# Second expert layer over sorted rows: dense experts replaced by 71 tiles of 128 rows of one expert

## What is computed

```python
x = x + window_attention(ln(x))                      # layer 0
t = x + experts0(ln(x))                              # 8 experts, top 2, renormalised gates
x = t + (whiten @ centred ln(t)) * gamma + beta      # layer 1: whitening by 3 Newton steps
# layer 1 experts: E = 8, H = 256, K = 2, on xf = ln(x), T = 4096 rows
probs = softmax(xf @ router_w + router_b)
topk_p, topk_i = top_k(probs, 2)                     # gates are these two, zero elsewhere
h = einsum('td,edh->teh', xf, w1) + b1
gated = silu(h @ wg + bg) * (h @ wv + bv)            # per expert, 256 wide
y = einsum('tef,efd->ted', gated, w2) + b2
out = einsum('ted,te->td', y, gates)
```

## Time and profile before

| | us |
|---|---|
| median of 3 runs | 1011.64 (1011.33 to 1014.1) |
| span of the profiled execution | 1014.5 |
| whitening matrix finished in it (end of L941) | 649.2 |
| first layer-1 expert matmul starts | 665.6 |

### The profile page before, as it was taken

The page is one execution under the profiler, slowest core; times in us unless marked ns, Lnnn a source line. Parts: engine busy times, 40 slices in busy tenths (PEclk is TensorE's granted clock), DMA queues, the critical chain, the costliest instruction groups (busy, mean ns, idle before and its releaser), DMA issues.

```text
span 1014.5 us, 18749 instructions
## 1 busy us (share of the span) xinstructions
PE 942.3 (93%) x6320; PEld 628.4 (62%) x6320; DVE 717.7 (71%) x1356; ACT 544.0 (54%) x866; POOL 564.8 (56%) x444
## 2 busy tenths in 40 slices
PE   6798999999999999999999997479999999999997
PEld 3465565665655656666656564357767767676675
DVE  3445657668576676775784554469899898998976
ACT  1232536636547457276474432147676676667764
POOL 5223365574564565655645543146767666677664
PEclk9797999999999999999999999579999999999999
DMA  6331000000000000000000000000000000000000
GB/s 242 104 100 68 1 2 1 1 2 1 3 1 3 2 1 2 1 2 1 2 1 1 1 1 0 0 1 1 11 1 11 11 0 10 0 10 0 10 11 11
DMA packets 4317, 16.07 MB, mean 16 GB/s; under 512 B 528, under 2 KB 656, under 8 KB 3856
## 3 DMA queue, kind: packets, MB, share of 16 engines
q1 hardware_dynamic: 3168, 12.20, 3.3%
q0 software_dynamic: 640, 2.10, 0.6%
q10 hardware_dynamic: 432, 0.76, 0.2%
HBM read 12.95 MB, written 2.10 MB: 15 GB/s over the span
## 4 chain that ended last, share of the span: by engine, by line
PE 71%; DVE 13%; issue 8%; ACT 4%; POOL 2%; DMA 1%; DVEq 0%; ACTq 0%; POOLq 0%
PE bank L1107 10%; PE bank L1082 10%; PE bank L1084 9%; PE bank L1083 9%; PE bank L988 7%; PE bank L1088 3%; PE bank L1103 3%; PE bank L997 3%; PE bank L1010 3%; DVE ym L647 2%; DVE hid_l L798 2%; PE bank L1104 2%; PE bank L1105 2%; DVE work L788 2%; PE bank L1173 1%
## 5 line engine op out<-in xcount | busy, mean ns | idle before, releaser
L456 POOL TENSOR_TENSOR work<-work 128x512 f32<-128x512 f32 x256 | 364.6, 1433 | 231.6 <-DVE work L792 115.9
L1082 PE MATMUL bank<-xh,Wh 128*128 128x512 f32 x512 | 235.3, 459 | 6.1 <-DVE work L788 3.8
L1084 PE MATMUL bank<-xh,Wl 128*128 128x512 f32 x512 | 201.9, 394 | 0.0
L1083 PE MATMUL bank<-xl,Wh 128*128 128x512 f32 x512 | 201.6, 394 | 0.0
L563 ACT ACTIVATE work<-bank 128x512 f32<-128x512 f32 x128 | 76.6, 598 | 155.3 <-PE bank L1084 153.9
L563 ACT ACTIVATE work<-bank,gv_bias 128x512 f32<-128x512 f32 x128 | 88.2, 689 | 108.7 <-PE bank L1084 107.9
L1107 PE MATMUL bank<-work,W 128*128 128x512 f32 x256 | 139.4, 627 | 6.1 <-ACT ob L588 4.8
L792 DVE TENSOR_TENSOR work<-work,bank 128x512 f32<-128x512 f32 x128 | 87.0, 684 | 77.0 <-ACT work L563 77.0
L798 DVE TENSOR_TENSOR hid_l<-work,hid_h 128x512 fp32r<-128x512 f32 x128 | 133.7, 1045 | 8.3 <-ACT hid_h L574 8.2
L431 POOL TENSOR_TENSOR Sx<-Sx,srec 128x1024 f32<-128x1024 f32 x32 | 61.9, 1933 | 119.3 <-DVE srec L688 119.3
L1082 PEld LDWEIGHTS bank<-xh,Wh 128*128 128x128 f32 x512 | 96.9, 189 | 45.6 <-issue 21.0
(11 more groups left out here) (167 smaller groups left out, 1463.4 us busy)
## 6 DMA issues: line engine op xcount, KB each, us to landing
work<-w1gv_dram SPq DMA_DIRECT2D x8, 640.0 KB, 4.0
work<-w_dram POOLq DMA_DIRECT2D x8, 256.0 KB, 3.3
W<-w_dram SPq DMA_DIRECT2D x2, 1024.0 KB, 6.3
out_dram<-X SPq DMA_DIRECT2D x8, 256.0 KB, 2.0
X<-x_dram SPq DMA_DIRECT2D x1, 1792.0 KB, 8.8
S<-small_dram ACTq DMA_DIRECT2D x1, 358.0 KB, 6.7
C<-const_dram SPq DMA_DIRECT2D x1, 356.0 KB, 5.9
qkv_w<-att_w_dram ACTq DMA_DIRECT2D x1, 320.0 KB, 4.5
```

Source lines behind the costliest of these rows:

```text
L456: pool.tensor_tensor(h2[:, u % 4, :], h[:, u % 2, :], csb[:, (u // FT) % 2, :], ALU.mult)\
L1082: mm(dst, wh, xh[:, p, :], start=True, stop=False)
L1083: mm(dst, wh, xl[:, p, :], start=False, stop=False)
L1084: last = mm(dst, wl, xh[:, p, :], start=False, stop=True)
```

## The change

The dense experts of layer 1 and `schedule_1` are gone. In their place `*_sparse` functions do this, all unrolled:

- Preparation is by units of 8 tiles (1024 tokens, two blocks). Its steps are listed in `PREP_STEPS`. Units 0 and 1 are prepared ahead of the first expert tile; unit 2 is spread over the steps 0 to 7 of the tile loop and unit 3 over 8 to 15. Each unit's two experts per token are picked on DVE (`pick_first`), the place of each row among the rows of its expert is counted by matmuls with a triangular matrix ("place"), and POOL writes each token's normalised row twice, once for each chosen expert, with its gate and its own address behind it, into a DRAM buffer `region` by 16 indexed DMAs of 128 rows. The last unit adds 8 such DMAs for padding.
- DVE makes a list of tiles (`dve_list`, 19 small operations on one partition): where each tile starts in `region`, and which expert it has. Groups of 8, 16, 16 and 31 tiles become free after units 0, 1, 2 and 3.
- SP loads each tile's 128 rows and its expert's b2 row into a ring of 8 buffers. PE and SP read start and expert from the list into registers, eight tiles at a time.
- For each tile PE transposes the rows, ACT and DVE split them, three matmuls of 512 columns make gate and value for 256 hidden columns, ACT applies silu, DVE multiplies by value and gate, PE transposes back, ACT copies, and two plain f32 matmuls with W2 give the output. DVE adds gate times b2, and POOL writes the 128 rows to their places in the DRAM buffer `results` by one indexed DMA.
- At the end SP reads `results` (4 MB), DVE adds two rows to each token, and SP stores.

In the set-up, the layer-1 bias goes into the fold: DVE first shifts w1 (`dve_w1`, four small operations for each expert) and `pe_fold` gets a third matmul with 8 rows; `pe_fold_bias` is gone and the filler matmuls run in its steps. The splitting of W2 is gone. Centring and normalising in layer 1 move from DVE to ACT. The core of the diff:

```diff
+MOE_GROUPS = (8, 16, 16, 31)
+TILES_MOE = sum(MOE_GROUPS)
+REGS = 8
+RING = 8
+PREP_STEPS = ("centre0", "centre1", "turn0", "turn1", "white0", "white1", "y0", "y1", "features0", "features1",
+              "logits", "route", "place", "list")
+PREP_AT = {2: (0, 0, 1, 1, 2, 2, 3, 3, 4, 4, 5, 5, 6, 7),
+           3: (8, 8, 9, 9, 10, 10, 11, 11, 12, 12, 13, 13, 14, 15)}
+        def sp_sparse(sp):
...
+                if t >= RING:
+                    sp.wait_ge(y_out[k], 16 * (t // RING))
+                sp.dma_start(rowbuf[:, k, :], region[bass.ds(starts[t % REGS], P), :]).then_inc(row_in[k], 16)
+                sp.dma_start(b2buf[:, k, :], b2[bass.ds(experts[t % REGS], 1), :].to_broadcast([P, P]))\
+                    .then_inc(row_in[k], 16)
+        def pool_step(u, name):
...
+                for j in range(UNIT):
+                    for k in range(2):
+                        at = where[:, u % 2, 2 * j + k:2 * j + k + 1]
+                        pool.indirect_dma_start(region, bass.IndirectOffsetOnAxis(ap=at, axis=0),
+                                                unit_rows(u)[:, j, k, :], None,
+                                                bounds_check=E * REGION + P - 1, oob_is_err=False)\
+                            .then_inc(sorted_in[u], 16)
+        def pool_sparse():
...
+                    pool.wait_ge(y_sb, t - 1)
+                    pool.indirect_dma_start(
+                        results, bass.IndirectOffsetOnAxis(ap=rowbuf[:, k, PLACE_AT:PLACE_AT + 1].bitcast(U32), axis=0),
+                        ysb[:, k, :], None, bounds_check=PAIRS - 1, oob_is_err=False).then_inc(y_out[k], 16)
+        def pe_rows(q):
+            if q >= 1:
+                pe.wait_ge(xl1_sb, q)
+            for t in range(2 * q, min(TILES_MOE, 2 * q + 2)):
+                pe.wait_ge(row_in[t % RING], 32 * (t // RING + 1))
+                last = nc.tensor.transpose(bank[:, TURN_X, (t % 2) * P:(t % 2 + 1) * P], rowbuf[:, t % RING, 0:P], ident)
+            last.then_inc(xt_ps, 1)
+        def pe_sparse():
...
+                    mm(bank[:, t % 2, :], low, wh, start=True, stop=False)
+                    mm(bank[:, t % 2, :], high, wh, start=False, stop=False)
+                    mm(bank[:, t % 2, :], high, wl, start=False, stop=True).then_inc(gu_ps, 1)
+                if t >= 2:
+                    r = t - 2
+                    pe.wait_ge(ht_sb, r + 1)
...
+                if t % 2 == 0 and t + 2 < TILES_MOE:
+                    pe_rows(t // 2 + 1)
+                if 1 <= t <= TILES_MOE:
+                    r = t - 1
+                    pe.wait_ge(hh_sb, r + 1)
...
+                for u, name in prep_steps(t):
+                    pe_step(u, name)
+        def dve_sparse():
...
+            for i in range(BLOCKS):
+                dve.wait_ge(fetched_in[i % 4], 16 * (i // 4 + 1))
+                for k in range(2):
...
+                    v.tensor_tensor(xb(i), xb(i), fetched[:, i % 4, :, k * P:(k + 1) * P], ALU.add).then_inc(x_sum, 1)
```

More of the change, by code:

```diff
@@ L63, in half_constants @@
     one = np.uint16(0x3F80)
-    return np.concatenate([np.eye(P), sel.reshape(P, E * P)], 1).astype(np.uint16) * one
+    before = np.triu(np.ones((P, P)), 1)
+    return np.concatenate([np.eye(P), sel.reshape(P, E * P), before, np.ones((P, P))], 1).astype(np.uint16) * one
+REGION = TOKENS + P
+PAIRS = 2 * TOKENS
+ROW, GATE_AT, PLACE_AT = 130, 128, 129
+OUT_OF_RANGE = 1 << 20
+UNIT = 8
+MOE_GROUPS = (8, 16, 16, 31)
+GROUP_AT = tuple(sum(MOE_GROUPS[:g]) for g in range(len(MOE_GROUPS)))
+GROUP_MAX = max(MOE_GROUPS)
+TILES_MOE = sum(MOE_GROUPS)
+REGS = 8
+RING = 8
 CONST_AT, CONST_WIDTH = {}, 0
@@ L88 @@
 WARM = 4
[L89 to L91 removed]
+DOWN_LAG = 2
 ATT_AT = 5
@@ L114, in side_fills @@
             order.append(f"C{s // FT}")
-        if post and s == POST_SLOT[layer]:
+        if post and s == POST_SLOT:
             order.append("post")
@@ L361, in over_tiles, with tile_values @@
             return row.unsqueeze(1).to_broadcast([P, BT, P])
-        def stream_block(n, layer):
-            return n - BLOCKS if layer else n
         block = ctx.enter_context(nc.Block())
+        def tile_values(engine, t, what, top):
+            g = max(k for k, at in enumerate(GROUP_AT) if at <= t)
+            first = t - GROUP_AT[g]
+            _, values = nc.values_load_multi_w_load_instructions(
+                todo[0:1, g, what, first:first + REGS], engines=(engine,), min_val=0, max_val=top,
+                skip_runtime_bounds_check_because="the list is clamped where it is made")
+            return values
+        def sp_sparse(sp):
+            for t in range(TILES_MOE):
+                if t in GROUP_AT:
+                    g = GROUP_AT.index(t)
+                    sp.wait_ge(sorted_in[g], 16 * (2 * UNIT + (E if g == len(MOE_GROUPS) - 1 else 0)))
+                    if g == 0:
+                        sp.wait_ge(region_set, 16)
+                    sp.wait_ge(todo_sb, g + 1)
+                if t % REGS == 0:
+                    starts = tile_values(mybir.EngineType.SP, t, 0, E * REGION)
+                    experts = tile_values(mybir.EngineType.SP, t, 1, E - 1)
+                k = t % RING
+                if t >= RING:
[3 more added lines that the diff above has]
+                    .then_inc(row_in[k], 16)
+            for k in range(RING):
+                sp.wait_ge(y_out[k], 16 * ((TILES_MOE - 1 - k) // RING + 1))
+            by_token = results.rearrange("(p t k) d -> p t (k d)", p=P, k=2)
+            for i in range(BLOCKS):
+                if i >= 4:
+                    sp.wait_ge(x_sum, 2 * (i - 3))
+                sp.dma_start(fetched[:, i % 4, :, :], by_token[:, i * BT:(i + 1) * BT, :])\
+                    .then_inc(fetched_in[i % 4], 16)
+            for i in range(BLOCKS):
+                sp.wait_ge(x_sum, 2 * (i + 1))
+                sp.dma_start(out[:, i * BT:(i + 1) * BT, :], xb(i)).then_inc(stored, 16)
+            sp.wait_ge(stored, 16 * BLOCKS)
         @block.sync
@@ L1028, in pe_att, with pe_prep @@
                 last.then_inc(att_full, 1)
[L1030 to L1049 removed]
+        def pe_prep(sp, n, s, p):
+            pe, mm, at = nc.tensor, nc.tensor.matmul, PREP_SLOT
             if s == at["turn"]:
@@ L1060, in pe_prep @@
                     last = mm(bank[:, SIDE, k * E:(k + 1) * E], ymT[:, k * P:(k + 1) * P],
-                              par(f"router{layer}"), start=True, stop=True)
+                              par("router0"), start=True, stop=True)
                 last.then_inc(side_full, 1)
@@ L1187, in pe_fold_bias @@
-            last.then_inc(bias_ps, 1)
+            i = 2 * u + int(name[-1]) if name[-1].isdigit() else None
+            if name.startswith("turn"):
+                pe.wait_ge(wy_sb, BT * (i + 1))
+                if i > 0:
+                    pe.wait_ge(fts_sb, i)
+                for k in range(BT):
+                    last = nc.tensor.transpose(bank[:, ATT0, k * P:(k + 1) * P], yc[:, k, :], ident)
+                last.then_inc(wt_ps, 1)
+            if name.startswith("white"):
+                pe.wait_ge(fts_sb, i + 1)
+                if i > 0:
+                    pe.wait_ge(x_wh, i)
+                for k in range(BT):
+                    last = mm(bank[:, ATT1, k * P:(k + 1) * P], fts1[:, k * P:(k + 1) * P], whiten,
+                              start=True, stop=True)
+                last.then_inc(wh_ps, 1)
@@ new lines, in pe_step @@
+            if name.startswith("features"):
+                pe.wait_ge(y1_sb, BT * (i + 1))
+                if i % 2:
+                    pe.wait_ge(turn_sb, i)
+                elif u > 0:
+                    pe.wait_ge(prefix_rd, u)
+                for k in range(BT):
+                    last = nc.tensor.transpose(bank[:, SIDE, k * P:(k + 1) * P],
+                                               unit_rows(u)[:, BT * (i % 2) + k, 0, 0:P], ident)
+                last.then_inc(turn_ps, 1)
```

736 lines of the change are left out of this document (495 added, 241 removed).

## The result

The changed kernel takes 1041.39 us (median of 4 runs, 1038.91 to 1046.32). The kernel before, on the same chip, takes 1012.87 (1011.33 to 1016.41). The ratio is 1.0284 with a 95% interval of 1.0246 to 1.0322: slower by 2.8%, where I had forecast 940 us. The profiled execution has a span of 1044.5, against the 943.2 of my sum.

A forecast was written before the change was run, and what follows sets the result against it. The prediction took layer 1 to be bound by PE's column count and summed 649.2 (up to the whitening matrix) + 86 (start) + 131 (tiles) + 52 (units 2 and 3) + 25 (end) = 943.2, so 940 us; range 890 to 1020.

The forecast's parts named there:

- w = 1.7: Expert tiles: PE's own work for one tile, 1.4 us plus 0.3 for gaps, makes 1.7 us.
- The formula of the ring: Expert tiles, eight buffers: time per tile is a quarter of PE's work plus the buffer's round trip; 1.8 us.
- L = 5.45: Expert tiles: a buffer's trip from one tile's W2 matmul to the transpose of the tile eight later takes 5.45 us.
- the ring's round trip is long: Rival, tiles: DRAM writes then reads and busy queues make the trip 9 us, a tile 2.7, total 994; chance 0.1.
- p = 1.2: POOL: one indexed DMA of 128 rows costs 1.2 us, some twice a plain one.
- The slope of 81 us for each us of p: Whole kernel: each us of an indexed DMA's price adds 81 us, from 64 exposed scatters and the tiles.
- Both rivals on p: POOL's indexed DMAs: dear at 2.4 us each, total 1051, chance 0.15; or cheap at 0.6, total 891, chance 0.15.
- The start, 86: From whitening matrix until two tile iterations are done, with units 0 and 1 prepared ahead: 86 us.
- The four terms 26, 19, 22 and 19: Start: unit 0's chain 26 us, its 16 scatters 19, the rest of unit 1's chain 22, its scatters 19.
- The weave, 52 on top of 1.9 a tile: Tiles with units 2 and 3 woven in: each unit adds 12 us of work and 14 of scatters, 52 together.
- The set-up, net 0, from -5 to +5: Before the whitening matrix: savings on PE and added fold work cancel, net 0 us, from -5 to +5.
- TensorE's clock as a rival: Rival, tiles: TensorE at its lower clock makes a tile 2.9 us and not 1.9, total 1009; chance 0.1.

The follow-up runs named there:

- e1: The changed kernel with a ring of 14 buffers instead of 8: 996.05 us, ratio 0.9851.
- e4: The changed kernel with b2 rows loaded once for each buffer and not for each tile, so b2 is wrong later: 1012.24 us, measured once.
- e9: The changed kernel with POOL's 143 indexed DMAs replaced by plain ones to fixed places, so nothing is sorted: 976.61 us, ratio 0.966.
- e13: e9 with fourteen buffers in the ring: 938.21 us, ratio 0.9262.
- e14: The changed kernel with fourteen buffers, reordered scatters, DVE's W1 work one step earlier, and three filler matmuls a tile up to tile 25: 970.36 us, ratio 0.9602.
- e5: The changed kernel with fourteen buffers, and units 2 and 3's scatters sent two behind each result row: 997.34 us, ratio 0.9832.
- e7: The changed kernel with DVE's centring of layer 1's W1 and its row means one attention step earlier: 1029.66 us, ratio 1.0186.
- e2: The changed kernel without DVE's four small operations for each expert (W1 centring, b1): 1020.7 us, ratio 1.0097.
- e8: The changed kernel without the third matmul of each W1 fold, so layer 1's gate and value biases are missing: 1033.66 us, ratio 1.0206.
- e11: The changed kernel with two extra bf16 matmuls of 512 columns on PE in each tile from tile 20 on: 1037.92 us, ratio 1.0254.

## Why the prediction was wrong, step by step

**What bounds the kernel before.** Nothing in the runs speaks against it.

**PE's work in a tile, w = 1.7.** Right: 1.55 to 1.72 in e1, 1.67 on average, and 1.73 for a tile when the ring is long.

**The formula of the ring.** Right in form. T = (w + L)/4 with w = 1.67 and L = 8.25 (odd tiles) gives 2.48, and SP's and PE's register loads every eight tiles come on top: measured 2.56. e4 and e9, each with a piece of L taken away, follow it: 1.92 by the formula and 1.94 measured, 2.26 and 2.34.

**Its term L = 5.45.** This is the step that failed for the steady tiles, and it is mis-sized by 2.8 us. POOL starts 0.84 after DVE is done, and I had a handover of 0.1; e9's plain DMA has 0.29 there, so most of this is once more a price of the index, which my p didn't hold. From POOL's start to SP's next issue 3.1, and I had p + 1.5 = 2.7. The loads need 0.52 for the second issue and 3.4 to land and set PE going, 3.9, and I had 2.3: this is the largest part. Three errors of one sign add up, and eight buffers have no slack for them. The term cost 35 us. My rival "the ring's round trip is long" (L = 9, T = 2.7, chance 0.1) was the mechanism that came true, nearly to its size; it had deserved the first place. I also priced it too low: with the 0.1 for registers that the base case has, its T is 2.8 and it costs 60 us and not 54. The rows I took the landing times from the earlier trace rows were of large transfers on quiet queues.

**The price of an indexed DMA, p = 1.2.** Right within 7%: 1.28 from start to start. The way to it was in part luck: the 1.02 us that I took for the price of single elements is the power on 128x4, while 128x512 elements of a multiplication take 1.43. The slope of 81 us for each us of p held in the total, where 0.75 less brought 65 us (61 by the slope). In its parts it held less well, so that the total is partly luck: up to tile 3 e9 gains 19 us (24 by the slope, for the 32 scatters of units 0 and 1), from there to tile 24 it gains 34 (28), and from tile 24 to the last result row 12 (9). Both rivals on p fell. The Trainium skill (DMA: Bandwidth & Descriptors, Anatomy of one DMA) calls descriptor generation small. For plain DMAs e9 agrees, with 0.53 from start to start. For indexed ones the measurement decides otherwise: 1.28 from start to start, so the index is over half of it.

**The start, 86.** Nearly right: the first tile came 75.4 us behind the matrix and not 73, tile 2 at 84.3. The four terms 26, 19, 22 and 19 measured 28.1, 20.4, 22.9 and 20.3, so that unit 1's scatters ended at 91.7 and not 86. These 6 us come out between tiles 2 and 3, where PE stands 8.2 us for DVE's addition (L1094), which needs POOL's addition from behind the scatters. They are part of the 8 us before tile 3 that the next paragraph names.

**The weave, 52 on top of 1.9 a tile.** This failed by 45 us. 21 of them are the two waits for bursts, which took 22.2 and 31.0 where I had 15.9 each. Ten of those are the eight DMAs for the regions' ends (8 x 1.28), which stand in the diff and which I didn't count. Ten more are what I let the ring hide, 5 of each burst. It did hide some: the burst began at 845.4 and PE waited from 853.6. But the row behind the burst, sent at 875.98, still had the rest of its trip before it, 6.3 us until PE went on, and I hadn't counted that. Another 16 are the 19 tiles between, with 4.0 us each and not 3.2. In e13, with plain DMAs and a long ring, these 19 still take 3.7 each, so more than half of this excess isn't the price of the index or the ring: the preparation of a unit costs the tiles more than the 12 us that I charged. PE runs there at a granted clock of 0.50 to 0.79 in the windows above; what part that has is not shown, since e14's fillers raised the clock and took time themselves. The last 8 lie before tile 3: 23.1 us where I had 14.9. With plain DMAs it takes 15.7 (e9) and 15.6 (e13), so these are POOL's scatters in the way.

**The set-up, net 0, from -5 to +5.** This failed too: +20 in the profile, and +12 to +21 over the nine profiles named under e5, all against the one profile of the kernel before. By the medians e7 gives 12 back by order alone, and e2 gives 21 back by leaving the work out. I had written that DVE's four small operations take 1 us for each expert and stand ahead of the fold, and had then set them against savings on PE. The step left out that PE, in its order, waits for them (11.2 us in six waits), and that PE then falls to its lower clock and needs twice the time for what follows. The extra passes of the fold were mis-sized beside it: 1.05 us for each expert at the higher clock, 8.4 in all, where I had about 4; e8 gives 7.7 back.

**TensorE's clock as a rival.** Its chance was 0.1, for the tiles. The granted clock there was 0.75 to 1.00, and e11 puts its price at some 0.1 us of a tile. For the steady tiles it fell. In the set-up, where I hadn't looked for it, it was real.

**The range.** 890 to 1020 had at its upper end one rival alone. The measured 1041 is the sum of three terms that each missed to the same side: 20, 45 and 35.

## What to carry to other kernels

Where a buffer goes round through several engines and DRAM, write the trip out with each handover and each landing of small transfers, and give the ring so many buffers that the trip fits, with room, into the work of the tiles between: going from 8 to 14 here was worth 45 us, and one small load less in the trip 29. Count the instructions of an in-order queue one by one, also those behind a loop: a burst of 24 at 1.28 us stops every engine that waits for what is queued behind it. A small operation put ahead of a matmul that has to wait for it costs its own time, the wait, and the clock that TensorE loses in the wait; one step earlier in the order gave back 12 us.

## What I had not expected of the hardware

An indexed DMA of 128 rows keeps POOL for 1.28 us from start to start, a plain one for 0.53, with the same rows and sizes. Between the end of DVE's operation and the start of POOL's DMA that waits for it lie 0.77 us when the DMA is indexed, and 0.29 when it is plain (e9). From POOL's start of an indexed write to DRAM to the next engine's instruction that waits for it lie 2.4 to 4.5 us (tiles 34 to 52), and a 64 KB row broadcast to 128 partitions took until 3.0 us behind its issue. And in a burst of indexed DMAs PE's semaphore updates are recorded up to 18.9 us behind their matmuls, and the engines that wait for them start as late, as told above; why stays open.
